# A selective-scan block on one core: a second row's turn, a gate product and the low halves in other slots

## The chip, the cores and the metric

The kernel runs on one core of a Trainium2 chip. A core has five engines that run their own instruction streams and meet at semaphores: TensorE (PE), VectorE (DVE), ScalarE (ACT), GpSimd (POOL) and SyncE (SP), the last of which issues most transfers here. The metric is the device time of one execution in microseconds (us).

## What is computed

The input x is 4096 tokens of 1024 channels. It goes through half a feed-forward step, a Mamba block and half a feed-forward step again, each behind a layer norm and each added to x:

```python
x = x + 0.5 * _L0_ffn_ref(_layernorm(x, axis=-1), L0_ffn_weight, L0_ffn_bias)
x = x + _L0_attn_ref(_layernorm(x, axis=-1), ...)
x = x + 0.5 * _L0_ffn_ref(_layernorm(x, axis=-1), L0_ffn_weight, L0_ffn_bias)
```

The feed-forward weight is ternary (-1, 0, 1 times a scale). The Mamba block is

```python
xz = x @ W_in.T
u, z = jnp.split(xz, 2, axis=-1)
...
dA = jnp.exp(dt[..., None] * A)
dBu = dt[..., None] * Bm[:, :, None, :] * u[..., None]

def step(h, inp):
    dA_t, dBu_t, C_t = inp
    h = dA_t * h + dBu_t
    y_t = jnp.einsum('bdn,bn->bd', h, C_t)
    return (h, y_t)
...
y = ys.swapaxes(0, 1) + u * Dskip
y = y * jax.nn.silu(z)
return y @ W_out.T
```

with 16 states n for each channel.

## The kernel before

The first pass, over 8 chunks of 512 tokens, does the first feed-forward step, the products for u, the convolution, dt, B and C, and writes x1, xz, y0, dt, dt*u, B and C to scratch tensors in memory. The change leaves it alone.

The second pass goes over 16 chunks of 256 tokens (two rows of 128 tokens, t = 0 and 1) and lies between 1085 us and the end. Each chunk has 16 **slots**, one for each state n. In the order of work that is written out by hand for each engine (`body(i, par)`), slot n does:

- GpSimd: `keep` (the carry of an earlier state), `times_b` (dbu = dtu_ times B; two products of half the channels each and a small addition of the carry), then `add_part` (an accumulating transfer that adds a part sum to y). dbu has two buffers.
- ScalarE: `decays`, p_da = exp(dt_ * A), in four pairs of two channel groups. There are two p_da banks, so pair p waits for scan p - 2. Behind them `part_state`, which multiplies the second row's turned state by C.
- VectorE: `scans`, four in a slot, 128x512 each: two, then `add_state` for the slot before (it adds the first row's turned state times C to y), then two more.
- TensorE: `turn_state`, 16 transposes of the state of the slot before into p_ht.
- SyncE: loads. `load_dt` for the next chunk is issued in slot 15, each of its four parts when that slot's decays have read the part of before; `load_dtu` likewise behind GpSimd's products.

The rest of the block is laid into the slots as **units** of TensorE, by the tables FFN, OUT and ZED, each unit in one of the two p_g banks by turns (`place` counts which bank and which use of it): z (the gate product, 24 matmuls), t (y turned), o (24 matmuls with W_out), n (the normalised row xn turned, 2 x 4 transposes), f (16 matmuls with the ternary weight). The second number is the row t, the third the half x. Chunk i does z for itself, t, o, n and f for chunk i - 1, and f of the second row for chunk i - 2, in its slots 0 and 1.

A turned row is needed in 16 bits as a high and a low half. `high` (ScalarE) copies the bank, TensorE's `take_high` subtracts that copy from the bank, `low` copies what remains and frees the bank. z is used by `tanh` (ScalarE) and `silu_part` (VectorE), which frees the bank; a p_g bank holding f is freed by `finish` (VectorE), one holding o by `add_product`. `gate`, `token_scale`, `mean_abs`, `scale_y` and `normalise` are the small steps between them.

Of the kernel before, what the change touches and what calls it, by code (L numbers as in the profile page):

```python
# [779 lines left out]
def second_pass(nc, sem, ins, tern, consts, ident, split_dram, dram, out):  # L780
# [6 lines left out]
    with ExitStack() as ctx:  # L787
# [33 lines left out]
        def banks(name, n, shape=(P, HALF)):  # L821
# [33 lines left out]

        FFN = {0: [("f", 1, 0)], 1: [("f", 1, 1)]}
        OUT = {4: [("t", 0, 0), ("t", 0, 1)], 5: [("o", 0, 0)], 6: [("o", 0, 1)], 7: [("t", 1, 0), ("t", 1, 1)],
               8: [("o", 1, 0)], 9: [("o", 1, 1)], 10: [("n", 0, 0), ("n", 0, 1)], 13: [("f", 0, 0)],
               14: [("f", 0, 1)], 15: [("n", 1, 0), ("n", 1, 1)]}
        ZED = {2: [("z", 0, 0)], 3: [("z", 0, 1)], 11: [("z", 1, 0)], 12: [("z", 1, 1)]}  # L860

        HALVES = {("t", 0): 0, ("t", 1): 2, ("n", 0): 4, ("n", 1): 6}

        def halves_before(i, n):

            return [(j, kind, t) for on, j, kind, t in
                    ((flags(i)[1] and n == 5, i, "t", 0), (flags(i)[1] and n == 8, i, "t", 1),
                     (flags(i)[1] and n == 11, i, "n", 0), (flags(i)[0] and n == 0, i - 1, "n", 1)) if on]

# [25 lines left out]
        def base(i):  # L895

            if isinstance(i, int) and i < 2:
                return i * 2
            if isinstance(i, int) and i == C2 + 1:
                return base(C2) + 8  # L900
            return (i - 2) * 10 + 11

        def place(i, kind, t, x):


            at = [u[1:] for u in sequence(i)].index((kind, t, x))
            return at % 2, base(i) + at // 2

        def more(i):

            return not (isinstance(i, int) and i >= C2 - 1)
# [10 lines left out]
        with nc.Block() as block:  # L922
            @block.sync
            def _(sp):
# [37 lines left out]
                def load_xz(c):  # L962
                    if not (isinstance(c, int) and c == 0):
                        b, m = place(c - 1, "z", 1, 1)
                        wait_alone(sp, g_full[b], m + 1)
                    for a in range(2):
                        sp.dma_start(xz[:, a].rearrange("p k t -> p (k t)"),
                                     dram["xz"][bass.ds(c, 1), a].rearrange("c p n -> p (c n)")).then_inc(xz_loaded, 16)
# [39 lines left out]
                def body(i, par):  # L1008
                    e_on, c_on, z_on = flags(i)
                    for n in range(NS):  # L1010
# [9 lines left out]
                        if z_on and edge(i) and n == 6:  # L1020
                            load_edge(i + 2)
                        if e_on and n in (1, 2, 3):
                            store(i - 2, *{1: (0, 1), 2: (1, 0), 3: (1, 1)}[n])
                        if c_on and n in (1, 7):
# [8 lines left out]
                        if z_on and more(i) and n == 9:  # L1033
                            load_y(i + 1, 1 - par)
                        if z_on and more(i) and n == 14:
                            load_xz(i + 1)
# [98 lines left out]
            def _(act):  # L1135
# [83 lines left out]
                def body(i, par):  # L1219
                    e_on, c_on, z_on = flags(i)  # L1220
                    c = i - 1
                    for n in range(NS):
                        for unit in halves_before(i, n):
                            low(*unit)
                        if z_on:
                            decays(i, par, n, (0, 1))
                        if c_on and n == 10:
                            normalise(i, c, 0)
                        if z_on and n in (3, 4, 12, 13):
                            tanh(i, n // 12, n - 3 if n < 12 else n - 12)  # L1230
                        if z_on:
# [5 lines left out]
                        if c_on and n == 0:  # L1237
                            part_state(i - 1, 1 - par, NS - 1)
                        if c_on:
                            if n in (2, 5):  # L1240
# [3 lines left out]
                            if n in (4, 7):  # L1244
                                high(i, "t", n // 7)
                            if n in (10, 15):
                                high(i, "n", n // 15)
                            if n == 14:
# [5 lines left out]
            def _(dve):  # L1254
# [35 lines left out]
                def silu_part(i, t, x):  # L1290

                    b, m = place(i, "z", t, x)
                    wait(dve, th_done, i * 4 + 2 * t + x + 1)
                    nc.vector.scalar_tensor_tensor(out=q[2 * t + x][:], in0=q[2 * t + x][:], scalar=1.0, in1=p_g[b][:],  # L1294
                                                   op0=ALU.add, op1=ALU.mult).then_inc(g_free[b], 1)
# [36 lines left out]
                def body(i, par):  # L1332
                    e_on, c_on, z_on = flags(i)
                    for n in range(NS):
                        if z_on:
                            scans(i, n, 0)
                            if n in (3, 4, 12, 13):
                                silu_part(i, n // 12, n - 3 if n < 12 else n - 12)

                        if c_on and n in (3, 6):  # L1340
# [7 lines left out]
                        if c_on and n in (6, 9):  # L1348
                            add_product(i, n // 9, 0)
                        if e_on and n in (1, 2):  # L1350
                            finish(i, i - 2, 1, n - 1)
                        if c_on and n in (14, 15):
# [13 lines left out]
            def _(pe):  # L1366
# [8 lines left out]
                def unit(i, par, kind, t, x):  # L1375
                    b, m = place(i, kind, t, x)
                    wait(pe, g_free[b], m)
                    cols = slice(x * HALF, (x + 1) * HALF)
                    n = 0
                    if kind in "tn":  # L1380
# [3 lines left out]
                        else:  # L1384
                            src = xn
                            wait(pe, xn_done, (i - 1) * TT2 + t + 1)
                        for k in range(4):
# [106 lines left out]
```

## Time and profile before

| | us |
|---|---|
| three runs | 2957.45, 2961.16, 3604.93 |
| median | 2961.16 |
| span of the profiled execution | 2958.3 |
| second pass in it, from VectorE's first instruction | 1085.3 to 2958.3 |

The page gives the profiled execution by its span alone, from the first instruction to the last; its own time isn't told apart from the three runs. A row of a timeline has its start, its length, engine, line and operation, the tile written and the tiles read, the number of instructions joined in it (x4), and in brackets the time for which the engine sat idle before it and what ended that. L1156 is ScalarE's decays, L1268 VectorE's scans, L1186 `high`, L1193 `low`, L1281 `add_state`, L1389 a unit that turns a row, L1415 a unit z, L1064 GpSimd's products, L1083 `add_part`.

### The profile page before, as it was taken

How to read it: one execution, taken by the hardware profiler on the slowest of the kernel's cores; microseconds unless marked ns; L12 is line 12 of the kernel's file. 1: busy time of each engine (PE TensorE's matmuls, PEld its weight loads, DVE VectorE, ACT ScalarE, POOL GpSimd, SP SyncE). 2: the span in 40 equal slices, each digit the busy share in tenths (PEclk: the TensorE clock that was granted, in tenths of full speed). 3: DMA queues.
4: the chain of work that ended last, by engine and by line, in shares of the span. 5: the costliest groups of instructions: out<-in, count | busy, mean ns of one | idle time of the engine just before them, and what ended most of it. 6: DMA issues, size and time to landing. Idle time of an engine off the chain costs nothing.

```text
span 2958.3 us, 37688 instructions
## 1 busy us (share of the span) xinstructions
PE 2439.5 (82%) x12448; PEld 1400.3 (47%) x12448; DVE 2378.5 (80%) x3197; ACT 2024.5 (68%) x3520; POOL 1874.5 (63%) x1673
## 2 busy tenths in 40 slices
PE   3577998998998736788888888888888889888897
PEld 1233444444443315555555555555555555555553
DVE  5566667677666649999999999999999999999992
ACT  2233766666766767778777777778777777777783
POOL 1112222222221138989989989989989989899991
PEclk8778999999999857889989999999989999999999
DMA  6454233233332256675675775676666766766744
GB/s 206 165 199 165 92 129 121 94 129 114 101 129 105 82 201 157 150 175 123 168 179 115 171 172 124 168 169 131 170 160 133 172 149 150 168 140 157 170 98 100
DMA packets 200290, 429.26 MB, mean 145 GB/s; under 512 B 44512, under 2 KB 93920, under 8 KB 199840
## 3 DMA queue, kind: packets, MB, share of 16 engines
q1 hardware_dynamic: 160928, 284.23, 29.1%
q0 software_dynamic: 39168, 142.62, 25.5%
q8 instruction: 100, 1.64, 0.2%
q14 instruction: 94, 0.77, 0.1%
HBM read 190.86 MB, written 110.10 MB: 102 GB/s over the span
## 4 chain that ended last, share of the span: by engine, by line
DVE 36%; PE 9%; ACT 7%; issue 6%; POOL 4%; DMA 1%; SPq 0%; DVEq 0%; POOLq 0%; ACTq 0%
DVE h L1268 25%; DVE y L1281 7%; PE p_g L1406 4%; POOL dbu L1064 3%; ACT p_da L1156 3%; PE p_ht L1372 2%; ACT tokt L1186 1%; ACT tokt L1193 1%; DVE x L1305 1%; PE p_g L1389 1%; ACT y_part L1173 1%; DVE q L1294 1%; DVE small L55 1%; DVE o L1315 1%; PE p_g L1415 1%
## 5 line engine op out<-in xcount | busy, mean ns | idle before, releaser
L1268 DVE TENSOR_TENSOR_SCAN h<-p_da,dbu 128x512 f32<-128x512 f32 x1024 | 1187.8, 1206 | 135.5 <-ACT p_da L1156 110.6
L1064 POOL TENSOR_TENSOR dbu<-dtu_,bb 128x1024 f32<-128x1024 f32 x512 | 1231.8, 2494 | 21.5 <-DMA dtu_<-dtu_scratch 20.9
L1156 ACT ACTIVATE p_da<-dt_,neg_a 128x255 f32<-128x255 f32 x2048 | 882.1, 467 | 331.8 <-DVE h L1268 325.9
L1372 PE MATMUL p_ht<-ident,h 128*128 128x128 f32 x4096 | 575.0, 300 | 131.5 <-DVE h L1268 128.6
L1372 PEld LDWEIGHTS p_ht<-ident,h 128*128 128x128 f32 x4096 | 520.6, 156 | 220.5 <-DVE h L1268 197.3
L714 PE MATMUL p_u<-xz,wu 128*128 128x512 f16 x1536 | 349.2, 385 | 8.2 <-DVE xz L508 6.2
L1406 PE MATMUL p_g<-wo,tokt 128*128 128x512 f16 x1536 | 350.7, 386 | 1.6 <-ACT tokt L1193 1.6
L1281 DVE SCALAR_TENSOR_TENSOR y<-p_ht,ct,y 128x1024 f32<-128x1024 f32 x272 | 344.3, 1266 | 8.0 <-PE p_ht L1372 7.7
L1415 PE MATMUL p_g<-wz,xz 128*128 128x512 f16 x1536 | 346.4, 382 | 0.0
L70 POOL TENSOR_TENSOR small<-small,consts 128x1 f32<-128x1 f32 x96 | 68.8, 717 | 423.9 <-DVE small L63 423.9
L363 POOL TENSOR_TENSOR late<-dt,u 128x512 f32<-128x512 f32 x64 | 81.6, 1274 | 376.9 <-DVE dt L561 376.9
L705 PE MATMUL p_ffn<-tern,xt 128*128 128x512 f16 x1024 | 254.6, 412 | 22.7 <-DVE xt L508 22.7
L1173 ACT ACTIVATE y_part<-p_ht,ct 128x1024 f32<-128x1024 f32 x224 | 245.3, 1095 | 7.8 <-PE p_ht L1372 6.9
L714 PEld LDWEIGHTS p_u<-xz,wu 128*128 128x128 f16 x1536 | 150.0, 99 | 200.6 <-issue 27.4
L1083 POOL DMA_DIRECT2D y<-y_part x224 | 202.0, 902 | 62.7 <-issue 36.3
L1406 PEld LDWEIGHTS p_g<-wo,tokt 128*128 128x128 f16 x1536 | 153.3, 100 | 176.7 <-issue 11.7
L1415 PEld LDWEIGHTS p_g<-wz,xz 128*128 128x128 f16 x1536 | 152.3, 99 | 170.6 <-issue 5.7
L1396 PE MATMUL p_g<-tern,tokt 128*128 128x512 f16 x1024 | 231.0, 379 | 1.6 <-ACT tokt L1193 1.6
L395 ACT ACTIVATE xn<-xin,small 128x1024 f32<-128x1024 f32 x32 | 39.7, 1241 | 238.6 <-POOL small L72 238.6
L693 PE MATMUL p_tr<-ident,xn 128*128 128x128 f32 x512 | 91.7, 338 | 125.3 <-DVE xt L508 75.7
L705 PEld LDWEIGHTS p_ffn<-tern,xt 128*128 128x128 f16 x1024 | 108.7, 106 | 158.6 <-issue 60.1
L1396 PEld LDWEIGHTS p_g<-tern,tokt 128*128 128x128 f16 x1024 | 100.1, 98 | 109.1 <-ACT tokt L1193 2.1
(117 smaller groups left out, 2862.0 us busy)
## 6 DMA issues: line engine op xcount, KB each, us to landing
y<-y_part POOLq DMA_DIRECT2D x224, 512.0 KB, 5.8
bb<-b_scratch SPq DMA_DIRECT2D x128, 256.0 KB, 3.6
xin<-in_x SPq DMA_DIRECT2D x32, 512.0 KB, 5.8
x_scratch<-x SPq DMA_DIRECT2D x32, 512.0 KB, 5.1
xz_scratch<-xz SPq DMA_DIRECT2D x16, 1024.0 KB, 6.2
y_scratch<-late SPq DMA_DIRECT2D x32, 512.0 KB, 5.4
dt_scratch<-dt SPq DMA_DIRECT2D x64, 256.0 KB, 2.1
dtu_scratch<-late SPq DMA_DIRECT2D x64, 256.0 KB, 2.4
```

The costliest lines, as they stand in the source:

```text
L705: mm = nc.tensor.matmul(p_ffn[h][:], xt[:, a, g, :], tern[:, g, h * HALF:(h + 1) * HALF], start=(g == 0 and a == 0), stop=(g == G - 1 and ...
L714: mm = nc.tensor.matmul(p_u[g % 2][:].rearrange("p (h t) -> p h t", h=2), wu[wa][:, kk, g * P:(g + 1) * P], xz[par][:, xa, :, kk, :], star ...
L1064: nc.gpsimd.tensor_tensor(state[:, 4 * f:4 * f + 4, :], dtu[:, 4 * f:4 * f + 4, :], bb[n // NB % 2][:, n % NB:n % NB + 1, :].to_broadcast( ...
L1083: pool.dma_start(into[:], part[part_of(c, n) % 3][:], accum_op=ALU.add).then_inc(done, 16)
L1156: ins_ = nc.scalar.activation(p_da[p % 2][:, k * T2 + 1:(k + 1) * T2], dt[:, g, 1:], ACT.Exp, scale=neg_a[:, g, n:n + 1])
L1173: nc.scalar.activation(into[:], p_ht[1][:], ACT.Copy, scale=ct[par][:, 1, n:n + 1]).then_inc(y_added[1], 1)
L1268: nc.vector.tensor_tensor_scan(h[n % 2][:, 2 * p:2 * p + 2, :].rearrange("p g t -> p (g t)"), p_da[p % 2][:], dbu[n % 2][:, 2 * p:2 * p + ...
L1281: nc.vector.scalar_tensor_tensor(out=y[par][t][:], in0=p_ht[t][:], scalar=ct[par][:, t, n:n + 1], in1=y[par][t][:], op0=ALU.mult, op1=ALU. ...
L1372: mm = nc.tensor.transpose(p_ht[t][:, g * P:(g + 1) * P], h[n % 2][:, g, t * P:(t + 1) * P], ident[:])
L1396: mm = nc.tensor.matmul(p_g[b][:], tokt[:, a, g, :], tern[:, g, cols], start=(n == 0), stop=(n == 2 * G - 1))
L1406: mm = nc.tensor.matmul(p_g[b][:], tokt[:, ta, g, :], wo[:, wa, g, cols], start=(n == 0), stop=(n == 3 * G - 1))
L1415: mm = nc.tensor.matmul(p_g[b][:], xz[:, xa, g, t * P:(t + 1) * P], wz[:, wa, g, cols], start=(n == 0), stop=(n == 3 * G - 1))
```

## The change

Three things move.

The second row's turn (n, 1) with its high halves leaves slot 15 for slot 0 of the next chunk, its low halves and the subtraction slot 0 for slot 1, and f of that row slots 0 and 1 for slots 1 and 2 (`finish` from slots 1 and 2 to 2 and 3, the stores behind it accordingly).

The first row's gate products leave slots 2 and 3 for slot 3 (half 0) and slot 15 (half 1). The tanh and silu of the latter are in slot 0 of the next chunk. `load_xz` waits for that product, so it goes from slot 14, behind z of slot 12, to slot 15, behind all dt_ loads.

On ScalarE every `low` stands behind the first two pairs of decays of its slot and no longer ahead of them.

```diff
@@ -853,11 +853,12 @@
-        FFN = {0: [("f", 1, 0)], 1: [("f", 1, 1)]}
+        FFN = {0: [("n", 1, 0), ("n", 1, 1)], 1: [("f", 1, 0)], 2: [("f", 1, 1)]}
         OUT = {4: [("t", 0, 0), ("t", 0, 1)], 5: [("o", 0, 0)], 6: [("o", 0, 1)], 7: [("t", 1, 0), ("t", 1, 1)],
                8: [("o", 1, 0)], 9: [("o", 1, 1)], 10: [("n", 0, 0), ("n", 0, 1)], 13: [("f", 0, 0)],
-               14: [("f", 0, 1)], 15: [("n", 1, 0), ("n", 1, 1)]}
-        ZED = {2: [("z", 0, 0)], 3: [("z", 0, 1)], 11: [("z", 1, 0)], 12: [("z", 1, 1)]}
+               14: [("f", 0, 1)]}
+        ZED = {3: [("z", 0, 0)], 11: [("z", 1, 0)], 12: [("z", 1, 1)], 15: [("z", 0, 1)]}
+        Z_NTH = {(0, 0): 0, (1, 0): 1, (1, 1): 2, (0, 1): 3}
...
-                     (flags(i)[1] and n == 11, i, "n", 0), (flags(i)[0] and n == 0, i - 1, "n", 1)) if on]
+                     (flags(i)[1] and n == 11, i, "n", 0), (flags(i)[0] and n == 1, i - 1, "n", 1)) if on]
...
                 def load_xz(c):
                     if not (isinstance(c, int) and c == 0):
-                        b, m = place(c - 1, "z", 1, 1)
+                        b, m = place(c - 1, "z", 0, 1)
...
-                        if e_on and n in (1, 2, 3):
-                            store(i - 2, *{1: (0, 1), 2: (1, 0), 3: (1, 1)}[n])
+                        if e_on and n in (1, 3, 4):
+                            store(i - 2, *{1: (0, 1), 3: (1, 0), 4: (1, 1)}[n])
...
-                        if z_on and more(i) and n == 14:
+                        if z_on and more(i) and n == 15:
                             load_xz(i + 1)
...
+                        if z_on:
+                            decays(i, par, n, (0, 1))
                         for unit in halves_before(i, n):
                             low(*unit)
-                        if z_on:
-                            decays(i, par, n, (0, 1))
                         if c_on and n == 10:
                             normalise(i, c, 0)
-                        if z_on and n in (3, 4, 12, 13):
-                            tanh(i, n // 12, n - 3 if n < 12 else n - 12)
+                        if c_on and n == 0:
+                            tanh(c, 0, 1)
+                        if z_on and n in (4, 12, 13):
+                            tanh(i, n // 12, n - 12 if n >= 12 else 0)
...
+                        if e_on and n == 0:
+                            high(i - 1, "n", 1)
...
-                            if n in (10, 15):
-                                high(i, "n", n // 15)
+                            if n == 10:
+                                high(i, "n", 0)
...
                         if z_on:
                             scans(i, n, 0)
-                            if n in (3, 4, 12, 13):
-                                silu_part(i, n // 12, n - 3 if n < 12 else n - 12)
-
+                        if c_on and n == 0:
+                            silu_part(i - 1, 0, 1)
+                        if z_on and n in (4, 12, 13):
+                            silu_part(i, n // 12, n - 12 if n >= 12 else 0)
...
-                        if e_on and n in (1, 2):
-                            finish(i, i - 2, 1, n - 1)
+                        if e_on and n in (2, 3):
+                            finish(i, i - 2, 1, n - 2)
```

The other lines of the diff count the units in their new places (`base`, `place`, `Z_NTH`, and the waits in `unit`).

ScalarE at the boundary of two chunks in mid-pass, from slot 15's decays to those of slot 2. p_da is a pair of decays (x4 is two pairs), tokt a high or low half, q a tanh, y_part a part sum. Before:

```order
L1156 ACTIVATE p_da<-dt_,neg_a 128x255 x8
L1173 ACTIVATE y_part<-p_ht,ct 128x1024
L1186 ACTIVATE tokt<-p_g 128x512 x2
L1193 ACTIVATE tokt<-p_g 128x512 x2
L1156 ACTIVATE p_da<-dt_,neg_a 128x255 x8
L1173 ACTIVATE y_part<-p_ht,ct 128x1024
L1156 ACTIVATE p_da<-dt_,neg_a 128x255 x16
```

And now:

```order
L1158 ACTIVATE p_da<-dt_,neg_a 128x255 x8
L1175 ACTIVATE y_part<-p_ht,ct 128x1024
L1158 ACTIVATE p_da<-dt_,neg_a 128x255 x4
L1182 ACTIVATE q<-p_g,consts 128x512
L1158 ACTIVATE p_da<-dt_,neg_a 128x255 x4
L1175 ACTIVATE y_part<-p_ht,ct 128x1024
L1188 ACTIVATE tokt<-p_g 128x512 x2
L1158 ACTIVATE p_da<-dt_,neg_a 128x255 x4
L1195 ACTIVATE tokt<-p_g 128x512 x2
L1158 ACTIVATE p_da<-dt_,neg_a 128x255 x12
```

The four halves no longer stand between the decays of slot 15 and slot 0; a tanh stands between the pairs of slot 0, the high halves behind them, the low halves between the pairs of slot 1.

SyncE at the same boundary, from the last bb loads of a chunk to the second bb load of the next. Before:

```order
L958 DMA bb<-b_scratch 128x512 x3
L967 DMA xz<-xz_scratch 128x2048 x2
L937 DMA dtu_<-dtu_scratch 128x1024 x2
L944 DMA dt_<-dt_scratch 128x512 x4
L1006 DMA out<-o 128x512
L958 DMA bb<-b_scratch 128x512
L1006 DMA out<-o 128x512
L976 DMA x_20<-x_scratch 128x1024
L958 DMA bb<-b_scratch 128x512
```

And now:

```order
L960 DMA bb<-b_scratch 128x512 x3
L939 DMA dtu_<-dtu_scratch 128x1024 x2
L946 DMA dt_<-dt_scratch 128x512 x4
L1008 DMA out<-o 128x512
L969 DMA xz<-xz_scratch 128x2048 x2
L960 DMA bb<-b_scratch 128x512
L1008 DMA out<-o 128x512
L978 DMA x_20<-x_scratch 128x1024
L960 DMA bb<-b_scratch 128x512
```

The xz loads, with their wait for the gate product of slot 15, went from ahead of dtu_ and dt_ to right ahead of the bb load for slots 2 and 3.

TensorE from slot 15's turning of the state (h) to slot 4. tern is f, wz a gate product, xn and minus_ident the second row's turn and its subtraction. Before:

```order
L1372 MATMUL p_ht<-ident,h 128x128 x16
L1389 MATMUL p_g<-ident,xn 128x128 x8
L1426 MATMUL p_g<-tokt,minus_ident 128x512 x2
L1372 MATMUL p_ht<-ident,h 128x128 x16
L1396 MATMUL p_g<-tern,tokt 128x512 x16
L1372 MATMUL p_ht<-ident,h 128x128 x16
L1396 MATMUL p_g<-tern,tokt 128x512 x16
L1372 MATMUL p_ht<-ident,h 128x128 x16
L1415 MATMUL p_g<-wz,xz 128x512 x24
L1372 MATMUL p_ht<-ident,h 128x128 x16
L1415 MATMUL p_g<-wz,xz 128x512 x24
```

And now:

```order
L1379 MATMUL p_ht<-ident,h 128x128 x16
L1422 MATMUL p_g<-wz,xz 128x512 x24
L1379 MATMUL p_ht<-ident,h 128x128 x16
L1396 MATMUL p_g<-ident,xn 128x128 x8
L1433 MATMUL p_g<-tokt,minus_ident 128x512 x2
L1379 MATMUL p_ht<-ident,h 128x128 x16
L1403 MATMUL p_g<-tern,tokt 128x512 x16
L1379 MATMUL p_ht<-ident,h 128x128 x16
L1403 MATMUL p_g<-tern,tokt 128x512 x16
L1379 MATMUL p_ht<-ident,h 128x128 x16
L1422 MATMUL p_g<-wz,xz 128x512 x24
```

The gate product that stood last in the list is now second, and the turn of xn comes one turning of the state later.

## Rows read from the trace of the kernel before

**Rows 1.** The page: busy time, share, instructions; VectorE's 40 slices.
```profile
PE 2439.5 (82%) x12448; PEld 1400.3 (47%) x12448; DVE 2378.5 (80%) x3197; ACT 2024.5 (68%) x3520; POOL 1874.5 (63%) x1673
...
DVE  5566667677666649999999999999999999999992
```

**Rows 2.** Waits of the second pass: us in total, times, longest.
```profile
DVE h L1268 <- ACT p_da L1156: 110.6, 72, 4.0
```

**Rows 3.** VectorE in order of time: first scans of slots 0 and 3, one chunk.
```profile
1994.29 2.34 DVE L1268 TENSOR_TENSOR_SCAN h<-p_da,dbu 128x512 f32<-128x512 f32 x2 [3.84 <-ACT p_da L1156]
...
2013.79 2.33 DVE L1268 TENSOR_TENSOR_SCAN h<-p_da,dbu 128x512 f32<-128x512 f32 x2
```

**Rows 4.** ScalarE in order of time, ahead of that slot 0.
```profile
1991.51 0.60 ACT L1186 ACTIVATE tokt<-p_g 128x512 f16<-128x512 f32 x1 [2.69 <-PE p_g L1389]
...
1992.80 0.60 ACT L1193 ACTIVATE tokt<-p_g 128x512 f16<-128x512 f32 x1 [0.21 <-PE p_g L1426]
1993.30 1.66 ACT L1156 ACTIVATE p_da<-dt_,neg_a 128x255 f32<-128x255 f32 x4
```

**Rows 5.** TensorE: a wait in slot 15, a gate product in slot 3.
```profile
1990.51 0.96 PE L1389 MATMUL p_g<-ident,xn 128*128 128x128 f32 x4 [4.55 <-DVE o L1315]
...
2015.09 5.34 PE L1415 MATMUL p_g<-wz,xz 128*128 128x512 f16 x24
```

**Rows 6.** VectorE, slot 0 of the first and last of 14 chunks.
```profile
1317.95 2.34 DVE L1268 TENSOR_TENSOR_SCAN h<-p_da,dbu 128x512 f32<-128x512 f32 x2 [3.99 <-ACT p_da L1156]
...
2782.09 2.34 DVE L1268 TENSOR_TENSOR_SCAN h<-p_da,dbu 128x512 f32<-128x512 f32 x2 [3.54 <-ACT p_da L1156]
```

**Rows 7.** VectorE, first scans of slots 5, 6, 8 and 11.
```profile
2027.92 2.34 DVE L1268 TENSOR_TENSOR_SCAN h<-p_da,dbu 128x512 f32<-128x512 f32 x2 [0.86 <-ACT p_da L1156]
...
2034.13 2.34 DVE L1268 TENSOR_TENSOR_SCAN h<-p_da,dbu 128x512 f32<-128x512 f32 x2 [0.45 <-ACT p_da L1156]
...
2048.57 2.34 DVE L1268 TENSOR_TENSOR_SCAN h<-p_da,dbu 128x512 f32<-128x512 f32 x2 [1.07 <-ACT p_da L1156]
...
2069.71 2.34 DVE L1268 TENSOR_TENSOR_SCAN h<-p_da,dbu 128x512 f32<-128x512 f32 x2 [1.07 <-ACT p_da L1156]
```

**Rows 8.** ScalarE, slots 4 and 5 of the same chunk.
```profile
2025.95 1.09 ACT L1193 ACTIVATE tokt<-p_g 128x512 f16<-128x512 f32 x2
2026.93 1.66 ACT L1156 ACTIVATE p_da<-dt_,neg_a 128x255 f32<-128x255 f32 x4
...
2032.10 1.04 ACT L1204 ACTIVATE xn<-y 128x1024 f32<-128x1024 f32 x1
...
2033.14 1.65 ACT L1156 ACTIVATE p_da<-dt_,neg_a 128x255 f32<-128x255 f32 x4
```

**Rows 9.** SyncE's dt_ issues; landing of the first (two chunks), us last.
```profile
1983.94 4.44 SPq L944 DMA_DIRECT2D dt_<-dt_scratch  x4
...
dt_<-dt_scratch SPq DMA_DIRECT2D x1, 256.0 KB, 8.1
...
dt_<-dt_scratch SPq DMA_DIRECT2D x1, 256.0 KB, 7.6
```

**Rows 10.** GpSimd, slots 0 to 3 of the chunk of rows 3.
```profile
1988.68 2.34 POOL L1064 TENSOR_TENSOR dbu<-dtu_,bb 128x1024 f32<-128x1024 f32 x1 [1.88 <-DMA dtu_<-dtu_scratch]
...
2000.14 0.20 POOL L1075 TENSOR_TENSOR carry<-h,carry_factor 128x8 f32<-128x8 f32 x1 [0.75 <-DVE h L1268]
...
2008.41 4.97 POOL L1064 TENSOR_TENSOR dbu<-dtu_,bb 128x1024 f32<-128x1024 f32 x2
2013.46 0.21 POOL L1069 TENSOR_TENSOR dbu<-dbu,carry 128x8 f32<-128x8 f32 x1
```

**Rows 11.** Slot 1 of the next chunk: a sum's landing; DMA share, GB/s (last).
```profile
y<-y_part POOLq DMA_DIRECT2D x1, 512.0 KB, 8.1
...
2110.00:2112.00 2.00, 1.01 (x5) 0.28 (x3) 2.00 (x3) 1.51 (x3) 0.81 (x1) 1.00 1.07 211
```

**Rows 12.** VectorE behind the last scan of all.
```profile
2895.12 1.28 DVE L1281 SCALAR_TENSOR_TENSOR y<-p_ht,ct,y 128x1024 f32<-128x1024 f32 x1 [4.28 <-PE p_ht L1372]
```

More of the change, by code:

```diff
@@ L900, in base @@
                 return base(C2) + 8
-            return (i - 2) * 10 + 11
+            return (i - 2) * 10 + 10
         def place(i, kind, t, x):
-            at = [u[1:] for u in sequence(i)].index((kind, t, x))
-            return at % 2, base(i) + at // 2
+            j = i + 1 if (kind, t) == ("n", 1) else i
+            at = [u[1:] for u in sequence(j)].index((kind, t, x))
+            return at % 2, base(j) + at // 2
         def more(i):
@@ L1292, in silu_part @@
                     b, m = place(i, "z", t, x)
-                    wait(dve, th_done, i * 4 + 2 * t + x + 1)
+                    wait(dve, th_done, i * 4 + Z_NTH[t, x] + 1)
                     nc.vector.scalar_tensor_tensor(out=q[2 * t + x][:], in0=q[2 * t + x][:], scalar=1.0, in1=p_g[b][:],
@@ L1375, in unit @@
                 def unit(i, par, kind, t, x):
-                    b, m = place(i, kind, t, x)
+                    b, m = place(i - 1 if (kind, t) == ("n", 1) else i, kind, t, x)
                     wait(pe, g_free[b], m)
@@ L1385, in unit @@
                             src = xn
-                            wait(pe, xn_done, (i - 1) * TT2 + t + 1)
+                            wait(pe, xn_done, (i - 1 - t) * TT2 + t + 1)
                         for k in range(4):
```

## Prediction

> **What bounds the kernel now.** I read the page first [rows 1]: VectorE (DVE) is busy for 80% of the span, and in the second pass nine tenths or more of every slice. The waits of that pass [rows 2] name what keeps it from the rest: before its scans it sat idle for 110.6 us, 72 times, until ScalarE (ACT) had written the decays. The timelines show where. In each of 14 chunks it waits ahead of the scans of slot 0, 3.99 us in the first and 3.54 in the last [rows 6], 3.84 in the one of rows 3; I take 3.8, in sum 53 us. The other 57 us lie at slots 5, 6, 8 and 11 of 15 chunks, 0.86, 0.45, 1.07 and 1.07 in one of them [rows 7] and 3.8 a chunk on average (57/15). Removing all of it is the most that the change can bring.
>
> The cause at slot 0: ScalarE waits 2.69 us for the second transpose of xn [rows 4], for which TensorE (PE) waited 4.55 us, until VectorE had emptied the bank [rows 5]; then come two low halves, and only then the decays that VectorE wants, at 1993.30. At slots 5, 8 and 11 the two low halves stand ahead of the decays too: 1.09 us for two [rows 8].
>
> I write T for the moment at which VectorE could start slot 0 if nothing held it: 1994.29 - 3.84 = 1990.45 in the chunk of rows 3.
>
> **The low halves behind the decays (slots 8 and 11).** Two halves cost 1.09 us and the wait is 1.07 us in both slots [rows 7, 8]. The halves now run beside the first two scans (2.33 us), while the next decays have to be ready only after a further sum, 3.4 us into the slot; two halves and one pair of decays are 1.1 + 0.9 = 2.0. So they are covered, and TensorE, which waits for them before its product, has its turning of the state (some 2 us) ahead anyway. I leave 0.2 us for slots 8 and 11 together.
>
> **Slots 5 and 6.** Here the cost only moves. The halves stand between the decays of slot 5 now, and behind them on ScalarE are two pairs, a part sum and the mean of |y| (1.04) before the decays of slot 6 [rows 8]. Decays for slot 5 could start at 2025.95 instead of 2026.93, but their second pair waits for the last scan of slot 4, which ends at 2027.92 - 0.86 = 2027.06; from there the same work reaches the decays of slot 6 about 0.55 us before the 2033.14 of rows 8. The stall of 0.86 + 0.45 = 1.31 becomes 1.31 - 0.55 = 0.8. GpSimd (POOL), which has a gate in this slot, has the input of slot 6 ready at about the same time and would hold it there in any case.
>
> So 3.8 a chunk becomes 0.2 + 0.8 + 0.2 for slots in which TensorE comes late = 1.2: a gain of 2.6 x 15 = **39 us**.
>
> **Slot 0: what is late next.** With the transposes gone ScalarE reaches the decays of slot 0 at once, but they read dt_, which SyncE's queue loads then. The first of its four loads is issued at 1983.94, that is T - 6.5, as soon as the decays of slot 15 have released the buffer, and lands 8.1 us later, 7.6 in the next chunk [rows 9]: T + 1.6 and T + 1.1. Today this is hidden under the wait for TensorE. A pair of decays (1.66/2 = 0.83) and 0.2 us of hand-over follow, so the first scan starts at T + 2.3. The stall goes from 3.8 to 2.3, not to zero: 1.5 x 14 = **21 us**.
>
> The gate product in slot 15 starts some 1.2 us after that slot does and takes 5.34 us [rows 5]; a slot is 6.3 us, so it ends at T + 0.2. Its tanh stands behind two pairs of decays, ending at T + 3.7; VectorE wants it at T + 2.3 + 2.3 = T + 4.6. No wait. The second transpose waits for the bank until T + 5.1, the high halves follow the last decays at about T + 6.5 and end at T + 7.6; VectorE starts slot 1 at T + 8.55, and its decays of 0.87 us just make it. Hence 0.
>
> **GpSimd on slots 0 to 3.** It has to multiply dbu for slot 3 before VectorE gets there. Its chain begins with the product that waits for dtu_ at 1988.68 (T - 1.8) and ends at 2013.46 + 0.21 = 2013.67, after only 0.75 us of waiting for VectorE [rows 10]; slot 3 starts at 2013.79 [rows 3], so its slack is 0.1 us. Without that 0.75 it ends at T + 22.5. VectorE needs 2013.79 - 1994.29 = 19.5 us from slot 0 to slot 3 [rows 3]; a silu has come and another work item gone, so 19.4: T + 2.3 + 19.4 = T + 21.7. New wait at slot 3: 0.8 us, x 14 = **-11 us**. It also means that an earlier dt_ would buy nothing, since GpSimd's chain starts from dtu_ and not from VectorE.
>
> **The transfers that move.** The two xz loads (1 MB) went out at slot 14; now SyncE holds them for the gate product, T + 0.2, and everything behind them: the bb load for slots 2 and 3, an output store and x1. GpSimd comes to that bb at T + 8.9. There is no row with this load behind 1 MB. The short bound is the 8.1 us of rows 9 and 11 from an issue at T + 1.1, T + 9.2: 0.3 us late. The long one is the 2 us stretch of rows 11: share 1.07, that is full, at 211 GB/s. If GpSimd's own sums take half, 1.5 MB at 105 GB/s are 14 us: T + 15, 6 us late. What GpSimd loses here comes back one to one at slot 3. I take 0.4 us a chunk, near the short bound because those 211 GB/s are measured with sums of both kinds in flight and plain loads were the smaller part: **-6 us**.
>
> GpSimd's own sums pay too: one lands 8.1 us after its issue in slot 1 as it is [rows 11], and 1 MB at 211 GB/s is 5 us of transfer time, the most by which they can be put off (rival 3). The Trainium skill, "DMA: Bandwidth & Descriptors", section "Issuing engines are not separate DMA queues", says that transfers of all issuing engines run on the same 16 DMA engines and interleave. By that rule alone the sums pay all of it and the time is the upper one of rival 3; by the order of issue (xz at T + 1, this sum at T + 8) most of xz is through by then. No row here shows the two together.
>
> **The end.** Behind the last scan VectorE waits 4.28 us for the turned state, behind the same transposes [rows 12]; they now come after it. The first product row of the tail waits for VectorE's finishing steps and gains about 2.5 us: **-2.5 us** of time.
>
> **Sum.** 39 + 21 + 2.5 - 11 - 6 = 45.5 us. The profiled span is 2958.3, against a median of 2961.2; the difference of 3 us lies around the span and stays. 2961.2 - 45.5 = **2915 us**, 1.5% faster; with contention from 0 to 1 us a chunk it is 2909 to 2924. About 2%, 59 us, is what a measurement of this kernel can tell from no change, and it is just above what I expect.
>
> **Rivals.**
> 1. The boundary is clean: dt_ and dtu_ land 2 us or more earlier, since nothing of xz is in flight before them, and GpSimd's chain starts earlier too. For it: dtu_ holds GpSimd for 1.88 us [rows 10]. Against: the xz loads of before were over 7 us before the first dt_ issue. GpSimd's chain then starts up to 1.9 us earlier and ends so much earlier at slot 3, which carries slot 0's saving through; with 0.3 us at slot 6 that is 45.5 + 6 + 14 x 2.2 = 82, so 2879.
> 2. ScalarE's 3.8 us at slots 5 to 11 return elsewhere, as the order of work there is only turned round: half of 39 is lost, and 2935.
> 3. The 1 MB delays the sums: GpSimd's merge in slot 2 waits 2 us for the sum before it, which lands 8.1 us after issue already while the gap is 8.4. Then 2 x 14 = 28 us come on top: 2943. All 5 us of it give 14 x 4.6 = 64 more than the forecast, 2979.
> 4. Slower: SyncE's bb load comes at the long bound, T + 15. Then 6.1 us are lost at slot 3 beside the 0.8: 6.1 x 14 = 85 in place of 6, 2961.2 + 34 = 2995. The change is a loss from a landing at T + 12.5 or so, where 0.8 + 3.6 eats the 62.5 us of gains.
> 5. TensorE: it now has a gate product in slot 15 and one fewer in slots 2 and 3. Its work per chunk is the same and the wait of 4.55 us is shorter; a bound on it would need over 6 us in slot 0, and I see 4.5.
>
> **Chances.** Forecast 0.55, rival 1 0.15, rival 2 0.1, rival 3 0.12, rival 4 0.08. The range from 2885 to 2955 leaves out the far part of rival 1, the far part of rival 3, and rival 4. Faster by over 2% (under 2902) comes from rival 1 and the edge of the forecast: 0.18; slower by over 2% (above 3020) 0.02; within 0.80.
>
> **What would show it.** In the profile after: VectorE's wait at slot 0 of about 2.2 us, with dt_ named as ScalarE's releaser; no wait at slots 8 and 11; about 0.8 at slot 6; about 1 us at slot 3 with GpSimd's dbu named; GpSimd waiting for bb or for a sum in slots 2 and 3 if contention is larger. The forecast is wrong if the wait at slot 0 stays near 3.8 or vanishes, or if GpSimd waits more than 3 us for bb in slot 2.

## The result and the profile after

| | us |
|---|---|
| after, median of 4 runs | 2986.18 (2984.7 to 2997.46) |
| before, median of 4 runs on the same chip | 2962.88 (2957.45 to 3604.93) |
| ratio, 95% interval | 1.0094 (1.0073 to 1.0115) |
| after, profiled execution: time, span | 2986.04, 2984.2 |

The kernel became 0.9% slower, where 1.5% faster was forecast. The time lies outside the range and on the other side. The run of 3604.93 us was in a slower state of the chip and is left out of the ratio.

VectorE's work did not change, as the page of the profile says: 2383.5 us against 2378.5 [rows 1]. What changed is the list of waits in the second pass. Each line has the waiting engine, its tile and line, what released it, then us in total, times and the longest.

```profile
DVE h L1274 <- POOL dbu L1071: 109.3, 53, 16.6
...
POOL dbu L1066 <- DMA bb<-b_scratch: 61.0, 15, 5.9
...
ACT p_da L1158 <- DMA dt_<-dt_scratch: 54.6, 23, 3.8
...
DVE h L1274 <- ACT p_da L1158: 35.1, 23, 2.7
```

VectorE's wait for ScalarE's decays fell from 110.6 us [rows 2] to 35.1. In its place it waits 109.3 us for dbu, GpSimd's product, and GpSimd waits 61.0 us, 15 times, for a load of bb, once at each boundary of two chunks. One boundary shows the chain. VectorE first, as in rows 3, then GpSimd, from slot 0 to slot 3 of a chunk in mid-pass:

```profile
2121.55 2.34 DVE L1274 TENSOR_TENSOR_SCAN h<-p_da,dbu 128x512 f32<-128x512 f32 x2 [2.45 <-ACT p_da L1158]
...
2137.20 2.34 DVE L1274 TENSOR_TENSOR_SCAN h<-p_da,dbu 128x512 f32<-128x512 f32 x2 [2.43 <-POOL dbu L1071]
...
2145.57 2.34 DVE L1274 TENSOR_TENSOR_SCAN h<-p_da,dbu 128x512 f32<-128x512 f32 x2 [1.97 <-POOL dbu L1071]
```
```profile
2117.00 2.36 POOL L1066 TENSOR_TENSOR dbu<-dtu_,bb 128x1024 f32<-128x1024 f32 x1 [1.31 <-DMA dtu_<-dtu_scratch]
...
2128.00 0.20 POOL L1077 TENSOR_TENSOR carry<-h,carry_factor 128x8 f32<-128x8 f32 x1 [0.30 <-DVE h L1274]
2132.22 4.67 POOL L1066 TENSOR_TENSOR dbu<-dtu_,bb 128x1024 f32<-128x1024 f32 x2 [4.02 <-DMA bb<-b_scratch]
```

T is 2121.55 - 2.45 = 2119.10 here. GpSimd comes to the bb of slots 2 and 3 at 2128.20, T + 9.1, and starts at 2132.22. VectorE pays for it at slot 2 (2.43 us) and slot 3 (1.97 us). SyncE's queue and the landings tell why bb is late:

```profile
2119.39 0.81 SPq L969 DMA_DIRECT2D xz<-xz_scratch  x2
2120.24 0.43 SPq L960 DMA_DIRECT2D bb<-b_scratch  x1
```
```profile
bb<-b_scratch SPq DMA_DIRECT2D x1, 256.0 KB, 11.9
```

Issued at 2120.24, right behind the two xz loads, it lands 11.9 us later, at 2132.1, which is T + 13.0. On the mean of chunks 2 to 14, counted from the traces, it takes 12.4 us (11.3 to 14.5), against 6.0 before.

ScalarE at the same boundary is where the plan was right. Its decays of slot 0 wait for dt_ and for nothing of TensorE:

```profile
2120.55 1.67 ACT L1158 ACTIVATE p_da<-dt_,neg_a 128x255 f32<-128x255 f32 x4 [3.57 <-DMA dt_<-dt_scratch]
```

VectorE's stall at slot 0 is 2.45 us, against 3.84 [rows 3]; on the mean of chunks 2 to 14 it is 1.83 against 3.87. At slots 8 and 11, where it was 1.07 each [rows 7], there is none in this chunk, and slot 6 keeps 0.86 us.

For the experiments one more view is needed. From the first scan of each slot to that of the next is the slot's length; this is its mean over chunks 2 to 14, counted from the traces. For e1, e4, e5 and e9 the traced run is the fastest of four, for e1 9 us below the median. A slot's length takes in the stall ahead of the slot behind it, so the stall at slot 0 stands under 15 and the one at slot 3 under 2. The kernels of the lower rows come below.

```
slot      0     1     2     3     4     5     6     7     8     9    10    11    12    13    14    15    sum
before  5.68  7.51  6.31  6.98  7.22  6.26  7.00  7.88  7.35  6.31  7.70  7.36  6.27  6.28  6.32 10.22 112.63
after   6.87  9.96  8.37  7.00  6.27  6.76  7.43  6.87  7.35  6.37  6.56  7.37  6.30  6.59  6.32  8.17 114.55
e4      7.51  7.97  8.30  7.00  7.31  6.21  7.26  7.89  7.35  6.31  7.58  7.37  6.29  6.34  6.32  8.59 115.58
e3      5.90  7.51  7.00  6.93  6.28  6.71  7.12  6.61  7.35  6.33  6.53  7.36  6.27  6.46  6.32  8.78 109.44
e7      5.68  7.51  6.37  6.96  6.28  6.68  7.11  6.54  7.35  6.38  6.59  7.36  6.27  6.54  6.32 10.03 109.97
e1      7.10  6.86  8.60  7.02  6.27  6.77  7.45  6.85  7.35  6.39  6.59  7.37  6.30  6.48  6.32  8.05 111.77
e5      6.95  6.86  7.38  7.00  6.27  6.80  7.63  7.02  7.35  6.37  6.54  7.37  6.30  6.51  6.32  8.10 110.77
e9      7.22  6.86  7.64  7.00  6.52  6.56  6.97  6.40  7.35  6.32  6.55  7.37  6.29  6.36  6.32  7.99 109.72
```

Slots 4, 7 and 10 shrank by 3.1 us a chunk together, slot 15 by 2.05, slots 0, 1 and 2 grew by 5.7, slots 5 and 6 by 0.9: 1.9 us a chunk more.

### The profile page after: what moved, and what is told of

It reads as the page before. It is cut to its first block, busy times and chain, and to the rows that moved or that the text cites. A ratio compares the mean times of both kernels' runs of the same rounds, so it can differ in the third digit from the quotient of the medians.

```text
span 2984.2 us, 37688 instructions
## 1 busy us (share of the span) xinstructions
PE 2444.2 (82%) x12448; PEld 1412.9 (47%) x12448; DVE 2383.5 (80%) x3197; ACT 2013.1 (67%) x3520; POOL 1875.2 (63%) x1673
## 4 chain that ended last, share of the span: by engine, by line
POOL 24%; DVE 17%; PE 12%; issue 7%; DMA 2%; ACT 1%; SPq 0%; POOLq 0%; DVEq 0%; ACTq 0%
POOL dbu L1066 19%; DVE h L1274 11%; PE p_g L1413 6%; PE p_ht L1379 4%; DVE y L1287 3%; POOL carry L1077 1%; POOL y L1085 1%; POOL y L1100 1%; DMA dt_<-dt_scratch 1%; PE p_g L1422 1%; DVE x L1311 1%; POOL dbu L1071 1%; PE p_g L1403 1%; DMA dtu_<-dtu_scratch 1%; POOL x L1104 1%
## 5 line engine op out<-in xcount | busy, mean ns | idle before, releaser
L1274 DVE TENSOR_TENSOR_SCAN h<-p_da,dbu 128x512 f32<-128x512 f32 x1024 | 1189.2, 1207 | 145.5 <-POOL dbu L1071 109.3
L1066 POOL TENSOR_TENSOR dbu<-dtu_,bb 128x1024 f32<-128x1024 f32 x512 | 1247.2, 2554 | 85.0 <-DMA bb<-b_scratch 61.0
L1379 PE MATMUL p_ht<-ident,h 128*128 128x128 f32 x4096 | 586.0, 305 | 172.2 <-DVE h L1274 172.2
L1379 PEld LDWEIGHTS p_ht<-ident,h 128*128 128x128 f32 x4096 | 536.0, 159 | 248.6 <-DVE h L1274 224.6
L1403 PE MATMUL p_g<-tern,tokt 128*128 128x512 f16 x1024 | 238.1, 387 | 2.3 <-ACT tokt L1195 2.3
```

The costliest lines, as they stand in the source:

```text
L1066: nc.gpsimd.tensor_tensor(state[:, 4 * f:4 * f + 4, :], dtu[:, 4 * f:4 * f + 4, :], bb[n // NB % 2][:, n % NB:n % NB + 1, :].to_broadcast( ...
L1274: nc.vector.tensor_tensor_scan(h[n % 2][:, 2 * p:2 * p + 2, :].rearrange("p g t -> p (g t)"), p_da[p % 2][:], dbu[n % 2][:, 2 * p:2 * p + ...
L1379: mm = nc.tensor.transpose(p_ht[t][:, g * P:(g + 1) * P], h[n % 2][:, g, t * P:(t + 1) * P], ident[:])
L1403: mm = nc.tensor.matmul(p_g[b][:], tokt[:, a, g, :], tern[:, g, cols], start=(n == 0), stop=(n == 2 * G - 1))
```

## The experiments

My theory after the result was A: xz's transfer ahead of bb costs the time, and the moves of the low halves and of the turn gain what I had said. Its rival B: the new order of the units costs it, and bb only shows where. Ten kernels ran; each is the kernel before or after with the edit shown. Ratios are to the kernel before on the same chip, with their 95% interval.

**e1: xz behind bb.** SyncE waits for the gate product and issues xz in slot 0 of the next chunk, behind the bb load.

```diff
                         if z_on and n % NB == 0:
 ...
+                        if z_on and i >= 1 and n == 0:
+                            load_xz(i)
 ...
-                        if z_on and more(i) and n == 15:
-                            load_xz(i + 1)
```

> The changed kernel with one edit on SyncE: the two xz loads are issued in slot 0 of the next chunk behind the bb load for slots 2 and 3, not ahead of it. Theory A (the 1 MB of xz ahead of that bb load is what costs): bb lands by T + 5, GpSimd's wait for bb (61 us in the changed kernel's trace) goes, VectorE's waits at slots 2 and 3 fall by 4 us a chunk, 14 to 15 times: 2986 - 57 = 2929 us, between 2920 and 2940. Theory B (slots 0 to 3 are set by dt_, by dtu_ and by GpSimd's own work, the bb wait only shows where GpSimd would have been late anyway): 2975 to 2986.

Measured: 2947.19 (2937.96 to 2950.48), ratio 0.9947 (0.9929 to 0.9965), 39 us below the kernel after. A stands, B falls, but the size is short. GpSimd's wait for bb is gone and another has come, at its merge at the end of slot 2, for the sum that it had issued before:

```profile
POOL y L1090 <- DMA y<-y_part: 19.5, 13, 3.6
```
```profile
2330.28 0.88 POOL L1090 DMA_DIRECT2D y<-y  x1 [0.96 <-DMA y<-y_part]
```

The megabyte now delays the sums, as rival 3 had it.

**e2: no xz transfer.** The kernel after without the xz loads of chunks 1 to 15. Its gate products use the first chunk's xz. SyncE still waits for the product.

```diff
                         wait_alone(sp, g_full[b], m + 1)
+                        return
```

> The changed kernel without the xz transfers of chunks 1 to 15 (z is computed from chunk 0's xz throughout); SyncE's wait for the gate product of slot 15 stays where it is. Theory A1 (the megabyte is the cost): bb is issued as late as in the changed kernel, T + 0.3, but lands within 8 us, GpSimd waits 0 to 0.5 us: 2920 to 2935 us. Theory A2 (the hold of SyncE's queue by the gate product is the cost): bb still comes after GpSimd gets there and GpSimd's wait stays above 2 us a chunk: 2960 or more.

Measured: 2930.72 (2923.72 to 2932.86), 0.9892 (0.9878 to 0.9907). The bytes are the cost, not SyncE's wait, with which bb is still issued late, at T + 0.3. It lands 5.1 us later on the mean of 13 boundaries (4.3 to 7.8), not 12.4. One of them:

```profile
bb<-b_scratch SPq DMA_DIRECT2D x1, 256.0 KB, 5.1
```

**e3: the low halves alone, on the kernel before.**

```diff
-                        for unit in halves_before(i, n):
-                            low(*unit)
                         if z_on:
                             decays(i, par, n, (0, 1))
+                        for unit in halves_before(i, n):
+                            low(*unit)
```

> The kernel before with the low halves behind the first two pairs of decays in their slot, and nothing else of the change. If this part is a gain by itself: slots 8 and 11 lose their waits (1.4 and 1.1 us a chunk), slots 5 and 6 keep 0.8 of 1.3, and slot 0 gains the two low halves of xn (1.2 to 1.8 us, then held by dt_): about 3.0 + 1.5 = 4.5 us a chunk, 2963 - 60 = 2903, between 2895 and 2925. Rival: the decays moved ahead only shift the waits by a slot, as the changed kernel's slots 5 and 6 show (0.9 us longer in sum): then 2930 to 2955.

Measured: 2918.64 (2917.25 to 2927.7), 0.9864 (0.9845 to 0.9883). 44 us faster than before, and 12 us faster than e2, which has all parts of the change and none of the transfer. So the turn's and the gate product's moves bring nothing even without the megabyte. The slot table shows the boundary: slots 15, 0, 1 and 2 of e3 sum to 29.2 us, those of e5 below to 29.3.

**e4: the moves alone.** The edit of e3 the other way round, on the kernel after.

```diff
-                        if z_on:
-                            decays(i, par, n, (0, 1))
                         for unit in halves_before(i, n):
                             low(*unit)
+                        if z_on:
+                            decays(i, par, n, (0, 1))
```

> The changed kernel with the low halves ahead of the decays again; the moved turn and gate product stay. In the changed kernel slots 4, 7 and 10 are 3.1 us a chunk shorter than before and slots 5 and 6 0.9 longer; if the low halves' place is the reason, this kernel gives those 2.2 us back and pays up to 1.1 at slot 1 as well: 2986 + 15 x 2.2 to 3.3 = 3019 to 3036. If GpSimd's lateness from the boundary hides part of it: 3000 to 3019.

Measured: 3011.67 (3005.34 to 3014.01), 1.0166 (1.0151 to 1.0182). The moves alone cost 50 us. The halves' new place gains 44 us on the kernel before and 25 on the one with the moves. Most of the difference lies at the boundary: slots 15, 0, 1 and 2 sum to 33.4 us in the kernel after and to 32.4 in e4. A VectorE that runs early meets a GpSimd that is late for bb there; that reading is argued from the table, not tried.

**e5: xz in slot 2.** As e1, but the loads go out in slot 2, some 9 us after T, when bb has landed. The sums of slots 0 and 1 are still under way.

```diff
+                        if z_on and i >= 1 and n == 2:
+                            load_xz(i)
 ...
-                        if z_on and more(i) and n == 15:
-                            load_xz(i + 1)
```

> The changed kernel with the xz loads issued in slot 2 of the next chunk, one slot ahead of the gate product that reads them, so that neither the bb load nor the sums of slots 0 and 1 meet them. Theory A (the megabyte delays first bb, then the sums): GpSimd's 19.5 us of waiting for a sum at its merge, left in the run with xz behind bb, goes, and slot 2 falls from 8.6 to 7.4 us: 2947 - 14 x 1.2 = 2930, the same as without the transfers (2931), between 2924 and 2938. Rival: the megabyte costs wherever it runs near the boundary: it stays at 2945 or more.

Measured: 2938.02 (2934.03 to 2940.53), 0.9920 (0.9905 to 0.9935). 48 us of the kernel after's time go with the same bytes three slots later. The wait at the merge is 6.4 us in all. That is the upper edge of what I expected, and still 19 us more than e3.

**e6: the transfer alone.** e3, in which SyncE holds xz until the last scan of slot 15, so that it goes out ahead of bb as in the kernel after; no unit is moved.

```diff
-                        if z_on and more(i) and n == 14:
+                        if z_on and more(i) and n == 15:
+                            wait_alone(sp, scan_done, (i + 1) * (NS * 4))
                             load_xz(i + 1)
```

> The kernel before with the low halves behind the decays (2919 us), and the xz loads held on SyncE until the last scan of slot 15 and then issued ahead of the bb load for slots 2 and 3; turn and gate product stay where they were before the change. Theory A: the transfers alone make the loss, GpSimd waits 3 to 4 us for bb at each boundary, slots 1 and 2 grow by as much: 2919 + 15 x 3 to 4 = 2964 to 2979. Theory C (the turn and the gate product in slots 0 and 15 make it): below 2935.

Measured: 2959.1 (2955.12 to 2967.93), 0.9992 (0.9983 to 1.0001), 40 us more than e3 with no unit moved. It is 5 us under the low end of theory A and 24 above the bound of C. GpSimd's wait for bb is back:

```profile
POOL dbu L1065 <- DMA bb<-b_scratch: 41.0, 14, 4.0
```

The transfer's place alone brings most of the loss. It was shown by taking it away (e2), moving it (e1, e5) and adding it (e6).

**e7: what slot 0 is worth.** e3 with the halves of slot 0 left ahead of the decays.

```diff
-                        for unit in halves_before(i, n):
+                        for unit in halves_before(i, n) if n == 0 else []:
                             low(*unit)
                         if z_on:
                             decays(i, par, n, (0, 1))
+                        for unit in halves_before(i, n) if n else []:
+                            low(*unit)
```

> The kernel before with the low halves behind the first pairs of decays in slots 5, 8 and 11, but still ahead of them in slot 0. It parts the 44 us of the low halves' edit into slot 0 and the others. By the slot lengths of the two traces (slots 4, 7, 10: 3.4 us shorter, slots 5 and 6: 0.6 longer) the others give 2.8 x 15 = 40 less what GpSimd's chain at slot 2 takes back, and slot 0 net 1.4 - 0.7 - 0.2 = 0.5 a chunk: 2919 + 7 = 2926, between 2920 and 2934. If slot 0 is worth its full 1.4 us a chunk: 2938.

Measured: 2921.51 (2919.45 to 2922.08), 0.9864 (0.9849 to 0.9879), 3 us more than e3 by the medians, with the same ratio, so the two are not told apart. Slots 5, 8 and 11 carry nearly the whole gain. In e3 the stall at slot 0 is 1.25 us shorter (8.78 against 10.03 under slot 15), slot 0 takes back 0.22 and slot 2 0.63 (7.00 against 6.37).

**e8: dt_ always there.** e5 without the dt_ loads of chunks 1 to 15, whose decays are computed from the first chunk's dt.

```diff
+                    if c:
+                        return
 ...
-                            wait(act, dt_loaded[p], i * 16 + 16)
+                            wait(act, dt_loaded[p], 16)
```

> The kernel with the xz loads in slot 2, and without the dt_ loads of chunks 1 to 15 (all chunks use chunk 0's dt_). Theory D (the end of slot 2 is set by GpSimd's chain from the dtu_ load on, so that an earlier dt_ buys nothing): slot 0's wait falls from about 2 us to 0.5 to 1, slot 2's grows by as much, and the time stays within 10 us of the run without this edit (about 2930). Rival (dt_ sets the boundary): 2930 - 14 x 1.5 = 2909 or less.

Measured: 2927.56 (2924.46 to 2932.07), 0.9891 (0.9874 to 0.9907). The loads of dt_, behind which ScalarE waits 3.57 us in the chunk shown above, are worth 10 us in all: the slot ahead of slot 0 falls from 8.10 us to 7.00, slot 2 takes 0.67 of it back (8.05 against 7.38). That is near what theory D allows and far from its rival's 2909. The edit takes away both the late landing and 1 MB of transfers a chunk, and does not part them.

**e9 and e10: the 19 us that were left.** e5 is slower than e3 in slots 6 and 7, by 0.9 us a chunk, far from the boundary. The windows of e5 by slot show why. The rows are slots 4, 5 and 6 of one chunk. Columns: the stretch, its length, then busy time (and instructions) of PE, PEld, DVE, ACT and POOL, the granted clock, the share of the DMA engines and GB/s.

```profile
2119.16:2125.43 6.27, 3.37 (x24) 2.27 (x22) 6.27 (x8) 5.57 (x11) 6.19 (x6) 0.94 0.55 125
2125.43:2132.38 6.95, 6.82 (x26) 4.71 (x27) 5.75 (x6) 6.47 (x14) 6.50 (x6) 0.56 0.40 116
2132.38:2140.67 8.29, 8.29 (x48) 4.74 (x47) 6.98 (x12) 5.63 (x11) 7.30 (x8) 1.00 0.39 80
```

In slot 4 TensorE is busy for 3.37 of 6.27 us, and the clock falls from 2.4 to 1.2 GHz: 0.56 is granted in slot 5. The product with W_out takes 6.57 us there and not 5.34, and VectorE's sum waits 1.24 us for the turning of the state behind it:

```profile
2129.03 6.57 PE L1413 MATMUL p_g<-wo,tokt 128*128 128x512 f16 x24
...
2136.58 1.28 DVE L1287 SCALAR_TENSOR_TENSOR y<-p_ht,ct,y 128x1024 f32<-128x1024 f32 x1 [1.24 <-PE p_ht L1379]
```

Over 13 chunks the clock of slot 5 is 0.96 on average before, 0.89 in e3 and 0.68 in e5; in e5 slot 6 lasts 8.3 us in the chunks with 0.56 and 7.0 in those with 0.81 or more. I took it as the theory and gave TensorE work in the gaps of slot 4: the 4 transposes of the turn (t, 0) are issued 4 times for half 0 and twice for half 1, with the same result. e9 is e5 with that, e10 is e3 with that.

```diff
-                        for k in range(4):
+                        times = (4, 2)[x] if (kind, t) == ("t", 0) else 1
+                        for k in list(range(4)) * times:
```

> The kernel after with its xz loads in slot 2, in which TensorE repeats the first row's turn of y in slot 4: the 4 transposes of half 0 are issued 4 times, those of half 1 twice (the same values into the same bank, no change of the output). That is 2.0 + 0.7 us of work in the gaps in which TensorE stood idle ahead of half 1 and ahead of the subtraction. The same kernel without it took 2938.02, the kernel before with only the low halves moved 2918.64; what lies between is in the traces 0.9 us a chunk in slots 6 and 7. Theory K (clock): the gate product that left slot 2 leaves TensorE idle for half of slot 4, its granted clock is then 0.68 on average in slot 5 (0.89 in the kernel without the moves), a transposing of the state takes 3.7 us instead of 1.9 to 3.1 and the product with W_out 6.57 instead of 5.34, and VectorE waits for it at slot 6. Then the granted clock of slot 5 rises to 0.9 or more, slot 6 falls from 7.63 to about 7.0 and slot 7 from 7.02 to 6.6, together 0.9 x 15 = 13 us: about 2925 (2920 to 2930). Theory S (the order of steps itself costs slots 6 and 7 the 0.9 us, whatever the clock): slots 6 and 7 keep 7.6 and 7.0, and the time stays 2938 (2934 to 2942), or rises by up to 5 from the added work.

> The kernel before with the low halves behind the first two pairs of decays, and the same repeated transposes in slot 4. There the clock of slot 5 is 0.89 on average, in 7 of 13 chunks 1.00, and slot 6 lasts 7.12 us, 6.97 where the clock is full. Theory K: slot 6 falls to 6.97, at most 0.2 to 0.3 us a chunk with slot 7, 2 to 4 us in all: 2914 to 2918. Theory S: 2918 to 2922.

Measured: e9 2920.35 (2919.86 to 2921.84), 0.9867 (0.9851 to 0.9884), 18 us less than e5; e10 2916.57 (2912.61 to 2918.68), 0.9851 (0.9837 to 0.9866). In e9 the clock of slot 5 is 1.00 in all 13 chunks, slot 6 lasts 6.97 and slot 7 6.40. The same product, one chunk:

```profile
2112.24:2118.51 6.27, 4.86 (x40) 4.04 (x38) 6.27 (x8) 5.57 (x11) 6.19 (x6) 1.00 0.55 125
2118.51:2125.16 6.65, 6.49 (x37) 3.81 (x38) 5.76 (x7) 6.54 (x14) 6.54 (x6) 1.00 0.46 121
```
```profile
2120.64 5.34 PE L1414 MATMUL p_g<-wo,tokt 128*128 128x512 f16 x24
```

More work on TensorE made the kernel faster, and the theory that the order of steps costs slots 6 and 7 falls. The gain is 18 us where 13 were expected. In e10 the 2 us of gain are what the clock theory gave, but its interval overlaps that of e3; e10 is the fastest kernel here, with e3 beside it.

## Why the prediction was wrong

**What bounds the kernel: right.** Both the waits and the places were those of the profile.

**The low halves, slots 5, 6, 8 and 11 (39 us): right.** e7, which moves only these, is 40 us faster than before (2961.58 in that job). The residue at slot 6, 0.8 forecast, is 0.86 us in the chunk shown and 1.00 on the mean.

**Slot 0 and GpSimd behind it (21 - 11 = 10 us): both terms near, their worth for the moves too high.** The stall was forecast as 2.3 us with dt_ named. In the chunk shown it is 2.45 with dt_ named, but this chunk is one of the longer ones: the mean is 1.83, and of the 14 boundaries with a stall VectorE waits for ScalarE at 9 and for GpSimd's dbu at 5. The loss at slot 3 was forecast as 0.8; with xz out of the way it is 0.99 (e5). But the halves alone, without the turn's move, take 1.44 of the 2.05 us from slot 15 (e3), and two thirds of what slot 0 gains is given back: e3 has 1.25 us less than e7 under slot 15, 0.22 more under slot 0 and 0.63 more under slot 2, and the latter is the stall at slot 3 that I had forecast. What is left, 0.4 us a chunk, is 6 us, the medians give 3, and the intervals of both runs are wider than that. The moves add nothing to it: slots 15, 0, 1 and 2 sum to 29.7 us before, 29.2 in e3, 29.3 in e5 and 29.7 in e9. "An earlier dt_ would buy nothing" was too strong: e8 gives 10 us for it, 0.7 a chunk, with the bytes of dt_ taken away as well.

**The transfers that move (-6 us): this step failed.** The bb load was put "near the short bound", T + 9.2. It landed at T + 13.0, on the mean at T + 13.6, near the long one, T + 15, and GpSimd waited 4.0 us at the boundary shown, not 0.3. By e5 the place of xz costs 48 us, by e6 40. The time of issue was right (T + 1.1). What was mis-sized is the time from there to the landing: 8.1 us, that of transfers with no megabyte right ahead of them, where 12.4 were measured on the mean. Without the megabyte it is 5.1 (e2), so the megabyte costs this load some 7 us, of which the forecast let 0.4 a chunk through.

The reason I gave was a rate of 211 GB/s in a stretch of 2 us with mixed traffic [rows 11]. What the load gets of that rate is the question. In the stretch from the xz issue to the bb landing the DMA engines are full and move 304 GB/s (columns as above). Below it stands the same stretch by queue: packets, MB, share of the 16 engines' time. SyncE's transfers are the hardware queue, GpSimd's the software queue; no other engine issues any here.

```profile
2119.40:2132.20 12.80, 8.12 (x44) 6.24 (x43) 10.65 (x10) 10.29 (x22) 8.10 (x9) 0.75 1.05 304
...
q1 hardware_dynamic: 1140, 2.70, 57.8%
q0 software_dynamic: 333, 1.19, 47.6%
```

SyncE's queue moved 2.70 MB in 12.8 us, 211 GB/s, the very rate that I had trusted. But xz and bb, 1.25 MB or 1.31 million bytes, are only half of that, 103 GB/s over 12.7 us. The other half is what SyncE issued around them: the last dt_ loads, output stores, x1 and the next bb. The long bound had the rate of xz and bb right, 105 GB/s, by luck: it halved 211 for GpSimd's sums, which do take nearly half of the engines' time here, but SyncE's queue has 211 beside them. It also took 1.5 MB; with the 1.25 MB of xz and bb it is 12.5 us, from T + 1.1 on T + 13.6. The Trainium skill, "DMA: Bandwidth & Descriptors", section "Issuing engines are not separate DMA queues", says that the transfers of all issuing engines run on the same 16 DMA engines and interleave. The rows agree: both queues take about half of the engines' time. I had used it only for what xz does to GpSimd's sums and not for what these do to xz and bb. How much of the 7 us is theirs and how much the queue's other transfers', no run parts.

**The end (-2.5 us): right.** From the start of the last scan of all to the end of the span it is 66.2 us after and 69.3 before. In e9, with the same order of units, it is 69.0, so the term is small against its scatter.

**The rivals.** Rival 4 is what happened: slower, bb near the long bound, and the change "a loss from a landing at T + 12.5". It gave 2995 with a chance of 0.08; 2986 was measured. That the two are so close is in part luck, since the rival holds no loss by TensorE's clock. Two bounds for the dearest unknown were 6 us a chunk apart, no row decided between them, and the range held one only. Rival 3's mechanism shows once xz is behind bb, in e1: 19.5 us at the merge. Rival 5 dismissed TensorE since its work per chunk is the same. Its work was, its clock was not, and that of slot 5 cost 18 us in e5 (e5 less e9). Rival 1 did not come: the first dt_ load takes 7.1 us on the mean against 7.6 before, the first dtu_ load 3.8 in both. Its counter-argument was right in kind, though the second xz load of before landed 5.9 us ahead of the first dt_ issue in the chunk of rows 3, and not over 7. Rival 2 fell with e7.

**The sum by the runs.** 2961.6 before, less 40 for the halves at slots 5, 8 and 11 (e7), less 3 for those at slot 0 (e3), plus 48 for the place of xz (after less e5), plus 18 for the clock of slot 5 (e5 less e9), plus 2 left for the turn and the gate product in their new slots (e9 less e3), gives 2986.6, against 2986.2 measured. The terms are differences between neighbours on one way from before to after, so that they add up proves none of them, and another way gives other terms: the halves are worth 44 us without the moves and 25 with them, and slots 6 and 7, which the clock lengthens, sum to 14.3 us in the kernel after, 14.7 in e5 and 13.4 in e9. The turn's and the gate product's move were not tried apart, since with one of them alone a unit would wait for a bank that is freed only behind it. Why the clock of slot 5 falls oftener with the moves is open too: slots 3 to 5 hold nearly the same units, and TensorE is busy for 7.0, 6.1 and 3.4 us in slots 2, 3 and 4 of e5 and for 6.9, 6.0 and 3.9 in those of e3. Slot 4 by itself does not tell it: with the same 3.83 us of work there on the mean, slot 5 is granted 0.93 in e7 and 0.77 in e1. My word for it in the expectation of e9, the gate product that left slot 2, was not tested; that the clock is the cause of the 18 us was.

## What to carry to other kernels

A transfer that an edit moves must be priced by what is issued behind it and by all that shares the DMA engines with it, its own queue's other transfers included, and where two bounds lie 6 us apart and the loss comes 15 times, both belong into the range. Ahead of a gain at one engine, ask which other engine has slack at the next meeting: here GpSimd had 0.1 us, and a stall shortened by 1.25 us a chunk was worth 3 us in all by the medians, which the noise doesn't tell from none. And where TensorE has a thin slot, read its granted clock in the next one before calling its load unchanged.

## What was unexpected of the hardware

The load of bb at the boundary landed 11.9 us after its issue behind the megabyte, and the two xz loads after 5.1 and 9.5 us. In the kernel before the same load at the boundary of rows 3, issued 1.5 us before T and with xz gone out earlier, landed after 6.1 us. That row of the DMA issues could have been read ahead of the prediction:

```profile
bb<-b_scratch SPq DMA_DIRECT2D x1, 256.0 KB, 6.1
```

6.1 us and the 10 us that 1.05 million bytes take at 105 GB/s are 16 us; with the 211 GB/s that I had trusted they are 11, which is nearly the 11.9 measured. Neither would have given 8.1. The runs put the megabyte between the two: 12.4 less 5.1 (e2) is 7.3 us.

TensorE with 3.4 us of work in a slot of 6.3 was granted less clock in the next slot (0.68 on average, 0.56 in the chunk shown); with repeated transposes in the same slot (4.86 busy) it was granted 1.00 in 13 of 13 chunks, and the kernel with the added work was 18 us faster. The Trainium skill, "TensorE: Matmul & The Clock Gate", section "What's actually happening", says that a clock gate sets the array's clock by how busy TensorE has been recently, at 1.2 or 2.4 GHz. The rows agree with its two levels, and here the price appears one slot behind the thin one, on another engine.
